# Five token mixes moved from VectorE to ScalarE and GpSimd

## What is computed

```
xa  = layernorm(x)
sx  = shift(xa) - xa
t   = tanh((xa + sx * maa_x) @ maa_w1)              # 5 groups of 32
m_j = t_j @ maa_w2[j]                               # j = w, k, v, r, g
x_j = xa + sx * (maa_j + m_j)                       # the five token mixes
w   = exp(-exp(time_decay + tanh(x_w @ decay_w1) @ decay_w2))
r, k, v = x_r @ Wr.T, x_k @ Wk.T, x_v @ Wv.T;  g = silu(x_g @ Wg.T)
s   = k v + w * s;  y = r (faaaa * k v + s)         # along the tokens, by head
x   = x + (groupnorm(y) * gn_w + gn_b) * g @ Wo.T
x   = x + channel_mix(layernorm(x))
```

## Time and profile before

| | |
|---|---|
| median of 3 runs | 911.98 us (911.55 to 914.36) |
| profiled execution: span from first to last instruction | 917.0 us |
| TensorE (PE) busy | 866.0 us |
| VectorE (DVE) busy | 563.9 us |
| ScalarE (ACT) busy | 429.6 us |
| GpSimd (POOL) busy | 227.8 us |
| mean granted TensorE clock | 0.977 |

### The profile page before, as it was taken

One profiled execution on the slowest core, in us unless ns is written; L12 is line 12 of the kernel. 1 busy time (PEld: TensorE's weight loads), 2 busy tenths in 40 slices (PEclk: granted clock), 3 DMA queues, 4 the chain that ended last, 5 costly groups with the idle time before them and its releaser, 6 DMA issues.

```text
span 917.0 us, 17166 instructions
## 1 busy us (share of the span) xinstructions
PE 866.0 (94%) x6636; PEld 676.8 (74%) x6636; DVE 563.9 (62%) x1310; ACT 429.6 (47%) x965; POOL 227.8 (25%) x242
## 2 busy tenths in 40 slices
PE   5787999999999988999999999999989999999998
PEld 5666777777768675676787777877767777888987
DVE  3478999999999989552333453333333364544754
ACT  3302333424242445344666686657655785333442
POOL 3545454555646459200000000000000000110100
PEclk9958999999999999999999999999989999999999
DMA  7638464554545452103103020202050222000200
GB/s 269 165 81 235 123 181 122 147 152 131 150 149 152 120 145 68 55 28 84 40 8 85 8 62 2 62 1 62 15 198 1 103 109 86 1 0 0 81 0 34
DMA packets 44424, 80.56 MB, mean 88 GB/s; under 512 B 21485, under 2 KB 27629, under 8 KB 42558
## 3 DMA queue, kind: packets, MB, share of 16 engines
q1 hardware_dynamic: 39742, 77.71, 29.0%
q10 hardware_dynamic: 4608, 1.84, 0.9%
HBM read 70.36 MB, written 9.18 MB: 87 GB/s over the span
## 4 chain that ended last, share of the span: by engine, by line
PE 46%; DMA 3%; ACT 2%; issue 1%; DVE 1%; SPq 0%; DVEq 0%
PE bank L1857 8%; PE bank L1844 8%; PE bank L1715 8%; PE bank L1721 7%; PE bank L1807 5%; PE bank L1799 3%; PE bank L1829 2%; PE bank L1763 2%; PE bank L1749 2%; DMA cx<-latc_scratch 1%; DMA w<-in_w 1%; ACT smb L1295 1%; PE bank L1817 1%; ACT pts L1303 0%; PE bank L1470 0%
## 5 line engine op out<-in xcount | busy, mean ns | idle before, releaser
L899 DVE CUSTOM_DVE_ANT_0 smb<-bank,mask 112x487 f32<-112x487 f32 x128 | 78.1, 660 | 125.8 <-issue 125.7
L692 DVE TENSOR_TENSOR_SCAN scan<-bank,scan 128x448 f32<-128x448 f32 x128 | 132.1, 1074 | 8.1 <-POOL scan L546 5.0
L1476 PEld LDWEIGHTS bank<-xj,front 128*128 128x128 f32 x1024 | 122.0, 199 | 9.8 <-issue 8.8
L543 POOL TENSOR_TENSOR scan<-scan,ks 128x896 f32<-128x896 f32 x64 | 124.1, 1939 | 3.0 <-DMA scan<-v_scratch 2.7
L1476 PE MATMUL bank<-xj,front 128*128 128x112 f32 x1024 | 124.1, 283 | 0.6 <-POOL xj L534 0.6
L1295 ACT ACTIVATE smb<-smb,nmax 112x487 f32<-112x487 f32 x128 | 88.3, 692 | 65.4 <-DVE nmax L899 64.9
L520 POOL TENSOR_TENSOR small<-small,neghalf 112x1 f32<-112x1 f32 x24 | 13.4, 558 | 371.1 <-DVE small L931 274.7
L699 DVE TENSOR_TENSOR scan<-scan,bank 128x896 f32<-128x896 f32 x64 | 68.9, 1079 | 2.9 <-PE bank L1476 2.1
L534 POOL TENSOR_TENSOR xj<-tmp,xa 128x448 f32<-128x448 f32 x40 | 42.4, 1061 | 90.8 <-DVE tmp L661 90.8
L1807 PE MATMUL bank<-ident,smb 112*122 112x112 f32 x512 | 57.3, 264 | 4.2 <-ACT smb L1295 3.9
L1116 ACT ACTIVATE bank<-ws 128x448 f32<-128x448 f32 x32 | 17.5, 548 | 91.5 <-DVE scan L692 78.1
(11 more groups left out here) (195 smaller groups left out, 1765.1 us busy)
## 6 DMA issues: line engine op xcount, KB each, us to landing
scan<-v_scratch SPq DMA_DIRECT2D x64, 448.0 KB, 5.7
cx<-in_ctxt SPq DMA_DIRECT2D x8, 750.0 KB, 5.2
raw_w<-in_wbig SPq DMA_DIRECT2D x4, 1024.0 KB, 7.9
w<-in_w SPq DMA_DIRECT2D x2, 2048.0 KB, 8.1
w<-in_w SPq DMA_DIRECT2D x1, 3328.0 KB, 10.9
tail<-in_wbig SPq DMA_DIRECT2D x3, 1024.0 KB, 9.2
front<-in_wbig SPq DMA_DIRECT2D x2, 1024.0 KB, 10.4
x_f<-in_x SPq DMA_DIRECT2D x8, 224.0 KB, 6.5
```

The costliest lines, as they stand in the source:

```text
L543: g.tensor_tensor(buf[:, :, :], buf[:, :, :], ks[b % 2][:, k:k + 1, 0:T].broadcast_to([P, VS, T]), ALU.mult).then_inc(s["a_ready"], 1)
L692: n = v.tensor_tensor_scan(flat, decay, flat, 0.0, ALU.mult, ALU.add)
L899: v.tensor_tensor_reduce(sm[r], bank[r][0:T, 0:NKEY], mask_b[b % 2][:, :], -1.0 / DH, 3e38, ALU.add, ALU.min, nmax[:, h:h + 1]).then_inc(s ...
L1476: i = t_.matmul(tiles(dst)[:, m, :], w[:, k, m * P:(m + 1) * P], x[:, k, :], start=k == 0, stop=k == NT - 1)
```

## The change

VectorE's function `mix` goes. In its place ScalarE gets `share`, which takes each adapter out of PSUM and adds `maa_j` (four activations with a bias, through `columns`), and counts a new semaphore `share_ready`. GpSimd's `mixed` first multiplies the share by `sx`, in place, and counts `mix_ready`, and then adds `xa` as before. In ScalarE's period the shares of V and K stand behind `adapter_tanh`, ahead of `norm_weights`, that of W behind `norm_weights`, that of R behind `second_columns`, and that of G behind `decay_logs`. In period -1 the share of W stands ahead of the turning of Wg. So that a semaphore is free, the loads of `gnv` count on the semaphore of `Wo`, and both who wait for it wait for all 48.

```diff
             def norm_vectors(i, n):
...
-                            sp.dma_start(gnv[p:p + HT, i, :], of[j, m]).then_inc(s["gnv_loaded"], 16)
+                            sp.dma_start(gnv[p:p + HT, i, :], of[j, m]).then_inc(s["wlate_loaded"], 16)
...
             def mixed(d, j):
+                pool.wait_ge(s["share_ready"], d * NMIX + j + 1)
+                g.tensor_tensor(tmp[:, j % 2], tmp[:, j % 2], sx[:, :, :], ALU.mult).then_inc(s["mix_ready"], 1)
                 pool.wait_ge(s["mix_ready"], d * NMIX + j + 1)
...
-            def mix(d, j):
-                dve.wait_ge(s["m_ready"], d * NMIX + j + 1)
-                if j >= 2:
-                    dve.wait_ge(s["xj_ready"], d * NMIX + j - 1)
-                for k in range(NT):
-                    i = v.scalar_tensor_tensor(out=tmp[:, j % 2, k, :], in0=tiles(MIX_BANK[j])[:, k, :],
-                                               scalar=V["maa_" + "vkwrg"[j]][:, k:k + 1], in1=sx[:, k, :],
-                                               op0=ALU.add, op1=ALU.mult)
-                i.then_inc(s["mix_ready"], 1)
...
-                if 0 <= i + 1 < B:
-                    mix(i + 1, MIX_V)
...
+            def share(d, j):
+                act.wait_ge(s["m_ready"], d * NMIX + j + 1)
+                if j >= 2:
+                    act.wait_ge(s["xj_ready"], d * NMIX + j - 1)
+                columns(tmp[:, j % 2], tiles(MIX_BANK[j]), None, "maa_" + "vkwrg"[j], "share_ready")
...
             def norm_weights(b):
                 act.wait_ge(s["yn_ready"], b + 1)
                 if b == 0:
-                    act.wait_ge(s["gnv_loaded"], 16 * 2 * NT * NT)
+                    act.wait_ge(s["wlate_loaded"], 16 * 3 * NT * NT)
...
                 if 0 <= i + 1 < B:
                     adapter_tanh(i + 1)
+                    share(i + 1, MIX_V)
+                    share(i + 1, MIX_K)
                 if i + 1 == 0:
+                    share(0, MIX_W)
                     turned_weight("Wg", "wg_loaded", "wg_turned")
                 if 0 <= i - 1 < B - 1:
                     norm_weights(i - 1)
+                if 0 < i + 1 < B:
+                    share(i + 1, MIX_W)
...
                 if 0 <= i + 1 < B:
+                    share(i + 1, MIX_R)
                     decay_tanh(i + 1)
                     decay_logs(i + 1)
+                    share(i + 1, MIX_G)
...
             def block_output(b):
                 if b == 0:
-                    pe.wait_ge(s["wlate_loaded"], 16 * NT * NT)
+                    pe.wait_ge(s["wlate_loaded"], 16 * 3 * NT * NT)
```

More of the change, by code:

```diff
@@ L246, in build @@
         decay = bank[6][:, 0:NT * T]
-        names = """vec_loaded wv_loaded wg_loaded gnv_loaded wv_turned wg_turned const_loaded s0_loaded wk_loaded
+        names = """vec_loaded wv_loaded wg_loaded wv_turned wg_turned const_loaded s0_loaded wk_loaded
             wr_loaded wlate_loaded raw_loaded ob_loaded
             xf_loaded xt_loaded xn_ready xnT_ready xa_ready
-            sx_ready xxx_ready tp_ready t_ready m_ready mix_ready xj_ready pv_ready pk_ready pr_ready pg_ready
+            sx_ready xxx_ready tp_ready t_ready m_ready share_ready mix_ready xj_ready pv_ready pk_ready pr_ready pg_ready
             vt_ready ks_ready th_ready gate_ready v_stored vb_loaded0 vb_loaded1 vb_loaded2 vb_loaded3 vb_loaded4 vb_loaded5
@@ L805, in period @@
                     own_values(i)
-                if 0 <= i + 1 < B:
-                    mix(i + 1, MIX_K)
                 if 0 <= i < B:
@@ L810, in period @@
                     scan_chunk(i, 5)
-                if 0 <= i + 1 < B:
-                    mix(i + 1, MIX_W)
                 if 0 <= i < B:
@@ L829, in period @@
                     times_r(i, 6)
-                if 0 <= i + 1 < B:
-                    mix(i + 1, MIX_R)
                 if 0 <= i < B:
@@ L834, in period @@
                     times_r(i, 7)
-                if 0 <= i + 1 < B:
-                    mix(i + 1, MIX_G)
                 if 0 <= i - 1 < B - 1:
```

## The result

The changed kernel takes **951.51 us** in the median (951.04 to 954.09), the kernel before, on the same chip, 911.79 us: a ratio of 1.044 (95% interval 1.041 to 1.047), 39.7 us slower. The forecast was 942.0 in a range of 926 to 956, slower with a chance of 0.90.

The account below looks back on a forecast made before the run. It took TensorE and VectorE both to be full in 100 to 320 us. Delay 18 + clock 12 + 0 gave +30 us on the median of 911.98: 942 us, range 926 to 956.

Parts of the forecast that it names:

- The order of ScalarE's queue: Shares V and K ahead of norm_weights on ScalarE: block output 3.0 us later in six periods, 18 us (16.8 to 22.8).
- `yg` 0.60 on VectorE: Step in the delay chain between norm_weights and block output: VectorE's gating of yg takes 0.60 us.
- The clock: TensorE's granted clock falls behind the 3.4 us idle before the block output: 2.0 us in six periods, 12 (0 to 17).
- rival (a): The delay without the clock: TensorE's clock stays up or falls now and then; 930 us, down to 926; chance 0.22.
- GpSimd's doubled work: One more two-input instruction per mix on GpSimd, 5.3 us a period; booked at nothing in the full periods.
- rival (c): GpSimd becomes the wait: late G product, TensorE waits before the turned input; 946 to 955 us; chance 0.11.
- The filling: Pipeline filling: first scan about 2 us later, VectorE skips two mixes, 2.1 us; booked 0, 4 us either side.
- The wait for the G product at the turned input: TensorE's turned input waits for GpSimd's G product: possible 0.7 us in each of six periods, nothing booked.
- The share R ahead of the decay tanh: ScalarE's share R, 1.09 us, fits ahead of the decay tanh: 0 to 0.2 us a period, 0 taken.
- VectorE's relief: VectorE loses 160 instructions, 41.9 us, 5.2 a period; booked at nothing, gain at most 5.8 us.
- the 48 transfers: norm_weights(0) and the first block output wait for all 48 loads, issued well before they are needed: 0.

Follow-up runs that it names:

- the spare matmuls: Changed kernel with eleven matmuls that nobody reads in TensorE's wait for yg, in six periods: 941.13 us.
- the best version: Changed kernel with norm_weights, rstd(2) and three more instructions moved, the two last periods reordered, 5 and 7 spare matmuls in the last: 914.55 us, ratio 1.004.
- the second profile: The kernel before, unaltered, profiled once more: span 908.8 us, time 910.52 us.
- the eleven runs: Eleven executions with the change, most of the filling left as it was by their edits: first reciprocal at 91.16 to 95.03 us, 93.2 in the middle.
- the run with the order alone: Changed kernel with ScalarE's norm_weights ahead of the shares V, K and W: 934.75 us, ratio 1.027.
- both moves: Changed kernel with norm_weights ahead of the shares V, K, W on ScalarE and rstd(2) between scan inputs 6 and 7 on GpSimd: 920.0 us, ratio 1.007.

## Why the forecast was right in its sign and short by ten

- **The order of ScalarE's queue: right, mis-sized.** The delay was to be 3.0 us in each of six periods; it was 3.8 (4.13 to 4.22 against 0.35), 22.8 us instead of 18. The shares took 2.06 us where 2.1 was said, `norm_weights` 1.62 where 1.58 was said. The step that failed is "`yg` 0.60 on VectorE": it measured 1.42 us, because GpSimd's new product runs at that moment. With GpSimd held back, 0.62. The period, forecast at 46 to 48 us, is 48.3 to 49.7 in the first five and 51.4 in the sixth.
- **The clock: right in size, in part by luck.** 2.0 us a period were said, 12 in all; the six block outputs were 12.1 us too long, and the spare matmuls gave back 10.4. But single ones were 1.4 to 3.1 us too long, and the 2.0 was only the middle between two prices from the filling, 1.2 and 2.8. That a burst behind an idle gap begins cold held in all six, and rival (a) fell; behind waits of 3.1 us, with only V ahead, it held in five of six.
- **GpSimd's doubled work booked at nothing: right in this kernel, for a reason named only in part.** In the six full periods TensorE waits for no `xj` and no turned input. But the forecast did not see that the late block output covers the small instructions behind the mixes in GpSimd's queue too. Once the order on ScalarE is mended, rstd(2) is 1.6 us late in every period. That is rival (c) in another place, and it is worth 934.75 - 920.0 = 14.8 us with the clock, after its own repair had cost some in the last period.
- **The filling booked at 0, give or take 4: wrong.** It cost 7.6 us in the pair of usual executions, 4.8 in the best version and about 6 over all runs. The first scan input came 2.2 us later than in the row that "about 2" was worked out from (34.03) and 4.0 later than in the second profile; VectorE's skipped mixes won nothing back. The wait for the G product at the turned input, which the forecast named for the full periods alone, is there in the filling: 4.34 us. TensorE is 4.0 us behind at the first sums, 6.4 at the second products and 10.2 at the turned input, and VectorE 7.6 at the reciprocal; how these delays add up to that was not taken apart.
- **The rest.** The share R ahead of the decay tanh was "0 to 0.2"; in the sixth period, behind ScalarE's first casts for the attention, TensorE's wait for dt is 1.58 us instead of 0.62. The last period was not booked: +2.8 us, from a gating that GpSimd's late work held (1.14 us) and a block output that ran at the lower clock (6.54 us). VectorE's relief at 0 was right as long as the order stayed: it pays 0.4 us a period once three more instructions are moved. No wait for the 48 transfers appears.

So the terms by spans are 22.8 + 12.1 for yg and the clock, less 1.0 for smaller waits that shrank, 7.6 and 2.8, less 0.8: 43.5. The forecast's 30 lacked 4.8 of the gating, the filling and the last period. What stays open: which of its delays makes the filling longer, and how much of the 7.6 us, where the eleven runs have 3.8 to 7.7, is the state of the clock in that one execution.

## What to carry to other kernels

When work moves to an idle engine, write down what stands behind it in that engine's queue and who waits for that, for every engine past which it moves; busy shares say nothing on it. An operation that reads two SBUF tensors on VectorE should be costed beside what GpSimd will run at that moment, not by its own row. Before costing the filling of a pipeline, look at a second execution: one profile of it may be 7 us off.

## What the runs showed of the hardware

- VectorE's gating of 128x448 with two operands in SBUF: 0.60 us alone, 1.43 beside GpSimd's product, behind whose end it ended by 0.48; GpSimd's sum then took 1.32 instead of 1.05.
- VectorE's normalisation of 112x512 with one tensor operand: 0.54 us alone, 2.03 to 2.31 beside GpSimd's scan input of 2.1 us. The section of the Trainium skill named above names, beside two inputs, a 2-port mode of VectorE as the other case of the lock; that this instruction runs in it no row here shows.
- A wait of TensorE of 1.6 us brought the granted clock down in two of six periods of the run with the order alone (periods of 49.59 and 50.46 us against 44.98); with both moves, without that wait, it stayed at 1.00 from 95 to 320 us. Behind waits of 3.06 to 3.15 us it fell in five of six periods, behind 4.13 to 4.22 us in six of six.
- Two executions of the kernel before reached their first full period 7.1 us apart, 94.54 and 87.40, with the same instructions.
